# Raw loads ahead of the first stores, and four instead of two table zeroings among them, in a two-layer attention and expert kernel

## The reference

```python
def attention(x, Wq, Wk, Wv, Wo, k_blocks, v_blocks, block_tables, kv_lens):
    q, k, v = project(x)                     # 8 heads of 64, 4 groups
    q, k = rope(rms(q)), rope(rms(k))        # at positions kv_lens + t
    k_blocks[blk, :, off, :] = k             # new rows go into the paged cache
    v_blocks[blk, :, off, :] = v
    k_all, v_all = k_blocks[block_tables], v_blocks[block_tables]
    p = softmax(where(window of 256 up to pos, q @ k_all.T / 16, -inf))
    return (p @ v_all) @ Wo.T

def ffn0(x, gate_w, W, atoms, expert_atom_weights, importance, mask_idx):
    top_w, top_idx = top_k(x @ gate_w.T, 2)
    weighted = (softmax(expert_atom_weights) @ atoms) * sigmoid(importance)
    # 4096 cells (row, column) of W get a per-expert addend
    return x @ W.T + segment_sum(x[:, cols] * vals(top_w, weighted), rows)

x = x + ffn0(attention(x), ...)
x = x + ffn1(lora_linear(x), ...)            # 8 experts, top 2, gelu
```

## Time and profile before

| | us |
|---|---|
| median of 3 runs | 1075.94 |
| lowest, highest | 1072.74, 1085.37 |
| profiled execution, its own time | 1075.94 |
| its span | 1073.8 |
| TensorE busy in it | 932.9 (87%) |
| VectorE, ScalarE, GpSimd busy | 546.2, 416.6, 365.4 |

### The profile page before, as it was taken

How to read it: one execution, slowest core, us unless ns; L and a number is a source line. 1 busy time by engine, 2 the same in 40 slices (tenths; PEclk the granted TensorE clock), 3 DMA queues, 4 the chain that set the end, 5 groups by cost and what they waited for, 6 DMA issues and landing times.

```text
span 1073.8 us, 18328 instructions
## 1 busy us (share of the span) xinstructions
PE 932.9 (87%) x4690; PEld 604.4 (56%) x4691; DVE 546.2 (51%) x2190; ACT 416.6 (39%) x1273; POOL 365.4 (34%) x475
## 2 busy tenths in 40 slices
PE   6999999988988987159899969995499999999994
PEld 2457655555554544124444438884477777777772
DVE  4777587776678886533334433555133333333331
ACT  3553465565565654011111112221344554445540
POOL 3666144666653331103334430434021212212121
PEclk9995899999999999669999989998699999999998
DMA  7955813343344253568777647983633243333430
GB/s 244 279 216 151 320 51 100 81 144 100 81 141 138 84 191 124 146 212 224 206 175 134 128 91 244 377 309 129 189 68 71 60 77 58 67 69 61 78 47 0
DMA packets 78503, 152.11 MB, mean 142 GB/s; under 512 B 16743, under 2 KB 26103, under 8 KB 76784
## 3 DMA queue, kind: packets, MB, share of 16 engines
q1 hardware_dynamic: 41264, 87.27, 25.0%
q0 software_dynamic: 24832, 42.71, 19.8%
q10 hardware_dynamic: 12352, 21.51, 6.1%
HBM read 94.05 MB, written 69.00 MB: 152 GB/s over the span
## 4 chain that ended last, share of the span: by engine, by line
PE 63%; DVE 14%; DMA 9%; issue 8%; ACT 2%; DVEq 2%; SPq 1%; POOL 1%; ACTq 0%; POOLq 0%
PE ps L680 51%; DMA acc<-R,tok_i 5%; PE ps L686 4%; PE ps L750 2%; DVE R L1537 2%; DVE R L1555 2%; DVE R L1526 2%; PE ps L738 1%; ACT R L1041 1%; DMA rows<-zrow 1%; DMA R<-rows 1%; PE ps L731 1%; DMA R<-in_x_t 1%; PE ps L782 1%; PE ps L773 1%
## 5 line engine op out<-in xcount | busy, mean ns | idle before, releaser
L680 PE MATMUL ps<-R 128*128 128x128 f32 (+4 forms) x2768 | 683.3, 403 | 15.9 <-DMA R<-in_x_t 10.4
L680 PEld LDWEIGHTS ps<-R 128*128 128x128 f32 x2768 | 419.0, 194 | 240.8 <-issue 219.2
L652 POOL DMA_INDIRECT out_x<-R,tok_i x39 | 60.5, 1551 | 253.0 <-DVEq L1883 164.9
L686 PE MATMUL ps<-ident,R 128*128 128x128 f32 x440 | 67.9, 287 | 75.9 <-DMA R<-rows 60.5
L686 PEld LDWEIGHTS ps<-ident,R 128*128 128x128 f32 x440 | 54.0, 147 | 109.8 <-issue 95.5
L579 POOL DMA_INDIRECT rows<-R,slot_i x64 | 66.8, 1043 | 133.3 <-ACT lg L1173 59.3
L1057 ACT ACTIVATE R<-R,nmx 128x384 f32<-128x384 f32 x128 | 78.4, 622 | 78.3 <-DVE nmx L1526 78.2
L652 POOL DMA_INDIRECT acc<-R,tok_i x39 | 60.5, 1552 | 134.1 <-DVE R L1792 124.4
L1526 DVE CUSTOM_DVE_ANT_0 R<-ps,R,q_scale 128x384 f32<-128x384 f32 x128 | 73.7, 612 | 36.3 <-issue 36.3
L1218 ACT ACT_TABLE_LOAD x18 | 23.1, 1283 | 148.5 <-PE ps L680 148.5
L738 PE MATMUL ps<-ident,R 128*128 128x128 f32 x384 | 56.6, 283 | 23.3 <-DVE R L1537 12.6
(11 more groups left out here) (282 smaller groups left out, 920.4 us busy)
## 6 DMA issues: line engine op xcount, KB each, us to landing
R<-rows SPq DMA_DIRECT2D x78, 258.0 KB, 3.3
R<-in_fc ACTq DMA_DIRECT2D x16, 1024.0 KB, 6.8
m_buf<-R SPq DMA_DIRECT2D x8, 1024.0 KB, 8.7
R<-m_buf SPq DMA_DIRECT2D x16, 512.0 KB, 5.0
R<-acc SPq DMA_DIRECT2D x32, 256.0 KB, 5.9
R<-in_x_t SPq DMA_DIRECT2D x4, 1024.0 KB, 9.0
R<-in_x_t SPq DMA_DIRECT2D x8, 512.0 KB, 3.5
new_kv<-R SPq DMA_DIRECT2D x16, 256.0 KB, 3.2
```

What stands on the lines that cost most here:

```text
L652: po.indirect_dma_start(out=sums[s], out_offset=bass.IndirectOffsetOnAxis(ap=tok_i[:, s:s + 1], axis=0), in_=y_sb[s], in_offset=None, boun ...
L680: m = pe.matmul(out, lhs(k), rhs(k), start=(k == 0 and first), stop=(k == KC - 1 and last))
L686: m = pe.transpose(out[:, k * P:(k + 1) * P], src[:, k * P:(k + 1) * P], ident[:])
```

## The change

On SP, the loads of the gates, `wo`, `w1`, `b_o`, the atoms and the mask are issued in one row behind `load_x(3)`, ahead of the first store, with `load_q(0)` between them. The zeroings among the stores are four (behind stores 2, 5, 8 and 11) instead of two (behind stores 8 and 10). After the stores, the waits for the first scores (`s_dot`) and for the first product with V (`s_pv`) go: the loads of `wo_t` and `w0_t` wait only for `pre_w` (the raw products), and `load_q(1)` and the last four zeroings follow them at once. On VectorE, two steps of `index_work` in period 0 come earlier: the steps run at j = 1, 2, 4 and 7 instead of 1, 4, 6 and 7.

```diff
             load_x(3)
+            sp.dma_start(gate0[:], d["gate0_t"].rearrange(chunked, p=P)).then_inc(S["raw_dma"], 16)
+            sp.dma_start(gate1[:], d["gate1"].rearrange(chunked, p=P)).then_inc(S["raw_dma"], 16)
+            sp.dma_start(raw_wo, d["wo"].rearrange(chunked, p=P)).then_inc(S["raw_dma"], 16)
+            sp.dma_start(raw_w1, d["w1"].rearrange(chunked, p=P)).then_inc(S["raw_dma"], 16)
+            sp.dma_start(raw_b, d["b_o"].rearrange(chunked, p=P)).then_inc(S["raw_dma"], 16)
+            for x in range(2):
+                sp.dma_start(atoms[64 * x:64 * x + 64, :], d["atoms"][:, NS // 2 * x:NS // 2 * (x + 1)]).then_inc(S["atoms_d"], 16)
             load_q(0)
+            sp.dma_start(mask_bc, d["mask_idx"].partition_broadcast(P)).then_inc(S["mask_d"], 16)
...
             for t in range(NT):
                 sp.wait_ge(S["p1o"], t + 1)
                 sp.dma_start(np_v[:, t, :], kv_out[t % 4]).then_inc(S4["p1k"][t % 4], 16)
-                if t == 0:
-                    sp.dma_start(gate0[:], d["gate0_t"].rearrange(chunked, p=P)).then_inc(S["raw_dma"], 16)
...
-                if t == 6:
-                    sp.dma_start(mask_bc, d["mask_idx"].partition_broadcast(P)).then_inc(S["mask_d"], 16)
-                if t in (8, 10):
-                    zero_cells(t // 2 - 4)
+                if t in (2, 5, 8, 11):
+                    zero_cells(t // 3)
...
-            sp.wait_ge(S["o_p1"], 1)
-            load_q(1)
-            sp.wait_ge(S["s_dot"], 1)
             sp.wait_ge(S["pre_w"], 1)
...
             sp.dma_start(w0_t, d["w0_t"].rearrange(chunked, p=P)).then_inc(S["att_w"], 16)
-            sp.wait_ge(S["s_pv"], 1)
-            for n in range(2, 8):
+            sp.wait_ge(S["o_p1"], 1)
+            load_q(1)
+            for n in range(4, 8):
                 zero_cells(n)
...
-                    if first and j in (1, 4, 6, 7) or B in (1, 2) and j in (1, 4):
+                    if first and j in (1, 2, 4, 7) or B in (1, 2) and j in (1, 4):
                         next(index)
```

## The result

| | us |
|---|---|
| changed kernel, median of 20 runs | 1086.24 |
| kernel before, median of 20 runs | 1075.88 |
| ratio of the two | 1.0083, 95% interval 1.0057 to 1.0108 |
| span of the profiled executions | 1082.2 after, 1073.8 before |

The changed kernel is slower by 0.83%, about 8.9 us. I had 1078.9 us, +3.0, with a range up to 1085; the ratio times the first median of before is 1084.9, so it stands at the range's edge (the changed kernel's own median is beyond it), still inside the 1% that I called "within". The loss is three times the forecast one. Three slow executions of the changed kernel (1095.29, 1648.09 and 1707.81 us) are left out of the ratio.

What follows compares the result with a forecast made beforehand. The opening was taken as bound by TensorE's tiles, then the tail of roots, scaling, rope and landing of the last store. Stall 2.5, gathers 0.5, index steps 0.1 and -0.1 gave +3.0: 1078.9 us, range 1073 to 1085.

Steps and rivals of the forecast that it cites:

- Nothing waits for the moved loads: Opening loads: no engine waits for any of the moved loads in the trace, so these edits gain nothing.
- The queue is served in order: SP's queue: the store of tile 0 waits for the 6.03 MB of loads now in front of it.
- T0: Time at which the store of tile 0 lands: taken as 50.5 us, between 46.4 and 55.0.
- T0 - 48.06: Delay of GpSimd's last root behind the late first store: 2.5 us, 0 at the lower end, 7.0 at the upper.
- VectorE's work behind is 5 us of index steps that the next waits swallow: VectorE behind the delayed rope of tile 4: 5 us of index steps, swallowed by the next waits.
- The gathers: Last gather of batch 0 beside the early weight loads: lands late for the key transposes, +0.5 us, ends 0 and 1.0.
- The index steps: VectorE in period 0: product step at j = 2 hidden but for +0.1 us, at most 0.6; edge step -0.1.
- the allowance for a slow queue: Upper end of the range: 7.0 us for the late last root and 1.0 for the gathers.
- Rival 1: Stores overtake the loads or T0 is under 48, so the tail is as before: 1076 us; chance 0.24.
- Rival 2: Queue served at the slow pace of before, T0 = 55, tail 7.0 late, gathers 1: 1084 us; chance 0.13.
- Rival 3: T0 over 53.2 opens a TensorE gap before tile 12, clock falls to 1.2 GHz: +16, 1092 us; chance 0.07.
- Rival 4: Moving zeroings out of 113 to 132 us gives back TensorE clock, 6.4 us less the stall: 1072 us; chance 0.06.

## Why the prediction was right, and where not

- **Nothing waits for the moved loads, so nothing is gained.** Right. With the loads early, but the buffers' waits and the index steps' price taken away, the kernel is at 1.0008, not under 1; with loads and index steps back, the rest of the change measures 0.9998.
- **The queue is served in order, T0 = 50.5.** Right in kind, 2.3 us too early, half a microsecond of it this execution's later start (`load_x(3)` leaves at 26.67, not 26.17): 52.8, inside 46.4 to 55.0. I had taken the middle of two bounds; this is most of what the stall has over its predicted 2.5 us. From the landing of `load_x(3)` (26.67 + about 5.1) to T0 are 21.0 us for 6.32 million bytes, 301 GB/s on the mean. The deep queue did reach 406 to 427 GB/s; the mean is pulled down by 40 to 45, at 213. By the landings (`w1` at 38.5, `b_o` at 41.4, the halves of the atoms at 43.4 and 45.7) those are the transfers of `b_o` and of the atoms. Which of the two shapes is the cause (rows of 512 B, or 64 partitions) wasn't tried. The slow stretch of before that I called "`w1` alone" also holds `b_o`, issued at 38.68, so it was no measure of a load like `w1`.
- **T0 - 48.06 for the last root.** Right: it gives 4.7 for the measured T0, measured 4.2, both with the half microsecond of the later start. And the free part is there in the trace: at T0 = 42.1 nothing is lost. The formula holds only where the next stores land right behind store 0. On ScalarE's queue store 0 landed at 47.4, where it gives nothing, but store 1 at 52.65, and the scores were 4.2 us late (ScalarE had lost 6.5 us to issuing there as well).
- **"VectorE's work behind is 5 us of index steps that the next waits swallow."** This step failed. VectorE had waited 11.8 us, and after T0 its row had no idle time to swallow anything, so `sparse_eq` was 6.1 us late and stood in front of the last two ropes. The price is small: 0.5 us more in front of the last store than GpSimd's roots explain (3.7 us behind the raw products' start for the last root, 4.2 for the store).
- **The gathers, +0.5 with an end at 1.0.** Landing 6.94 against the assumed 6.3; TensorE waits 1.2. Right in kind, as the run with the wait back shows (2.7 us without the transfers beside it); undersized.
- **The index steps, +0.1, at most 0.6.** This term failed most, by its ratio. I read its cover, a projection of 4.62 us and the copy behind it, off one execution, and didn't see that this cover was itself TensorE at half clock (the earlier trace rows say 0.50 for 80 to 85, the trace up to 106). In the changed kernel the scores come 6 us later, the projection runs at 3.70 and full clock, and VectorE owns j = 2. The trace has 2.5 us more with the steps moved (B 79.2 against 76.7), the four pairs of timed runs 2.5 on the mean.
- **The sum.** Predicted 2.5 + 0.5 + 0.1 - 0.1 = 3.0. By the timed runs: 6.2 us for what the buffers release (stall, VectorE behind it and the gathers' wait) and 3.4 for the index steps, against 8.9 for the whole; that the two don't add up exactly is within their noise, and the run that undoes both is at 1.0008. The mechanism of the stall was right and its size too small; that the time still lies in the range is owed to the allowance for a slow queue (7.0 + 1.0), and not to the terms that failed. In that it was luck.
- **The rivals.** Rival 1 fell by the wait of 10.7 us. Rival 2, 1084, was nearest in time, but by another way: T0 was 52.8 and not 55, and VectorE and the index steps made up the rest. Rival 3 didn't come, as T0 stayed 0.4 under its point of 53.2 and TensorE had no gap there. Rival 4 had no part: the zeroings went out of the crowded stretch, and nothing came back. In the trace with raw loads and index steps back the DMA share is 0.00 in 116 to 122 and the granted clock 0.50 all the same.

## What to carry to other kernels

A load moved ahead of stores isn't free because nobody waits for it: ask which buffer the store behind it must release, and from what moment that costs. Here a first store that landed at 42.1 cost nothing and one at 52.8 cost 4.2 us in front of the last store; the point in between from which it costs, about 48, is computed and not measured. Another queue didn't help; more buffers did, in trace and timing, and half of the bytes did in the trace. When a stall is shifted onto an in-order engine, list everything in that engine's row up to the critical piece, and not only its idle time before. And a cover made of TensorE's work is to be priced at both of its clock levels.

## What was not expected of the hardware

- A 256 KB store in a queue of its own took 10.3 and 14.2 us beside more than 5 MB of loads in another queue, against 2.0 us at the least and 3.2 at the median of the 16 stores of before.
- TensorE's granted clock came back to 1.00 at about 101 us in four executions, at 106 to 111 in nine, and in one only at about 123, behind the long wait, with the same work in front of it in some of them; 2 us of VectorE's work cost nothing or 4 us along with it. What sets the moment stays open.
- Root 7 of GpSimd took 7.8 us beside `sparse_eq` in the kernel before, single steps up to 1.00 us where they take 0.20 elsewhere. With nothing of `sparse_eq` beside it, it took 5.1, in two kernels otherwise the same. The Trainium skill (SBUF — State Buffer, section Who interferes with whom) describes one port pair that VectorE and GpSimd lock against each other, for VectorE operations with two SBUF inputs too, where GpSimd's operation reads SBUF. The trace agrees: `sparse_eq` has two such inputs, one of its four parts takes about 0.97 us, and the steps beside it take 0.81 to 1.00.
